# Weight products placed one pair earlier, their loads ahead of the small ones, and a block end without GpSimd's drain

## What is computed

```
w = weights[conditions]                        # per sequence, 64 x 64
u = einsum('bct,bcd->bdt', x, w)
x = x + selective_scan(u, ...)                 # 16 states per channel
a = attention(x)                               # paged keys/values, window 256, 8 heads, 4 groups
a = a @ Wo
scores = a @ w_r + b_r;  idx = top_k(scores, L/2)
h = gelu(a[idx] @ w1 + b1)
out = zeros.at[idx].set(h @ w2 + b2)
x = x + out
```

## Time and profile before

| | us |
|---|---|
| runs of the kernel: median of 3 (lowest, highest) | 1920.51 (1919.56, 1924.25) |
| the profiled execution, its own time | 1921.25 |
| its span, from first to last instruction | 1919.4 |
| PE busy in the span | 1828.5 (95%) |
| DVE, ACT, POOL busy | 1457.0, 1261.0, 1267.4 |
| mean granted TensorE clock (1.0 is 2.4 GHz) | 0.986 |

### The profile page before, as it was taken

The page is one execution under the profiler, slowest core; times in us unless marked ns, Lnnn a source line. Parts: engine busy times, 40 slices in busy tenths (PEclk is TensorE's granted clock), DMA queues, the critical chain, the costliest instruction groups (busy, mean ns, idle before and its releaser), DMA issues.

```text
span 1919.4 us, 29987 instructions
## 1 busy us (share of the span) xinstructions
PE 1828.5 (95%) x9311; PEld 1273.0 (66%) x9311; DVE 1457.0 (76%) x2572; ACT 1261.0 (66%) x3937; POOL 1267.4 (66%) x1253
## 2 busy tenths in 40 slices
PE   7899999999999999988599899999999999999998
PEld 6777777777777777765355575756657575665765
DVE  8999999999999999997455565655656565565522
ACT  5888888888888888865354674655646465564621
POOL 5789999999999999988677545444554544550000
PEclk8999999999999999999799999999999999999999
DMA  5423322333233323320776434434353343431021
GB/s 205 151 107 145 144 112 113 139 142 126 103 139 145 145 96 123 132 88 24 221 211 200 113 89 112 123 108 124 93 141 100 108 122 108 123 95 60 30 64 42
DMA packets 117069, 228.57 MB, mean 119 GB/s; under 512 B 31332, under 2 KB 70260, under 8 KB 111920
## 3 DMA queue, kind: packets, MB, share of 16 engines
q1 hardware_dynamic: 83824, 161.38, 23.8%
q0 software_dynamic: 33088, 65.28, 12.6%
HBM read 209.99 MB, written 44.70 MB: 133 GB/s over the span
## 4 chain that ended last, share of the span: by engine, by line
PE 46%; ACT 2%; issue 1%; DMA 1%; DVE 1%; POOL 0%; DVEq 0%; SPq 0%; ACTq 0%; POOLq 0%
PE attn_psum L1911 12%; PE attn_psum L1927 11%; PE attn_psum L1843 5%; PE attn_psum L1823 5%; PE attn_psum L1830 4%; PE attn_psum L1869 3%; PE attn_psum L1814 2%; PE attn_psum L1945 2%; PE attn_psum L1804 1%; PE attn_psum L1855 1%; ACT xh L1556 1%; ACT th L1557 1%; DMA kv_at<-kv_scratch,new_now 0%; ACT prob L1514 0%; ACT k_t L1504 0%
## 5 line engine op out<-in xcount | busy, mean ns | idle before, releaser
L996 DVE TENSOR_TENSOR_SCAN hid<-scan_psum,dbu 128x1024 f32<-128x1024 f32 x256 | 581.7, 2273 | 0.0
L1161 PE MATMUL scan_psum<-hid,ident 128*128 128x256 f32 x2048 | 520.3, 385 | 26.4 <-POOL hid L492 26.2
L1161 PEld LDWEIGHTS scan_psum<-hid,ident 128*128 128x128 f32 x2048 | 378.8, 191 | 188.9 <-issue 106.4
L1665 DVE CUSTOM_DVE_ANT_0 prob<-attn_psum,mask 128x336 f32<-128x336 f32 x256 | 120.1, 505 | 280.8 <-PE attn_psum L1823 280.5
L492 POOL TENSOR_TENSOR hid<-hid,kv_at 128x1024 f32<-128x1024 f32 x128 | 306.2, 2404 | 27.5 <-DVE hid L996 27.2
L492 POOL TENSOR_TENSOR hid<-hid,bc 128x1024 f32<-128x1024 f32 x128 | 306.0, 2403 | 23.2 <-DVE hid L996 22.8
L1520 ACT COPY p_t<-attn_psum 112x384 f32<-112x384 f32 x256 | 122.3, 484 | 285.4 <-PE attn_psum L1830 285.4
L1927 PE MATMUL attn_psum<-w,ffn_hid 128*128 128x512 f32 x512 | 238.5, 595 | 5.0 <-DVE y_sb L1730 5.0
L1446 POOL DMA_INDIRECT kv_at<-kv_scratch,new_now x189 | 200.5, 1061 | 63.6 <-issue 56.7
L1911 PE MATMUL attn_psum<-xs_in,w 128*128 128x256 f32 x1024 | 232.4, 381 | 7.5 <-ACT xs_in L1526 6.6
L635 ACT ACTIVATE scan_psum<-kv_at,neg_a 128x252 f32<-128x252 f32 x512 | 211.6, 466 | 13.9 <-DVE hid L996 12.3
(11 more groups left out here) (222 smaller groups left out, 3036.2 us busy)
## 6 DMA issues: line engine op xcount, KB each, us to landing
bc<-bc_scratch SPq DMA_DIRECT2D x16, 2048.0 KB, 7.4
kv_at<-bc_scratch SPq DMA_DIRECT2D x15, 2048.0 KB, 7.4
q_scratch<-qg SPq DMA_DIRECT2D x32, 260.0 KB, 2.0
early<-q_scratch SPq DMA_DIRECT2D x32, 260.0 KB, 3.5
x_pair<-in_x_pairs SPq DMA_DIRECT2D x32, 256.0 KB, 2.8
kv_scratch<-kvg SPq DMA_DIRECT2D x32, 256.0 KB, 2.1
a_scratch<-a_sb SPq DMA_DIRECT2D x32, 256.0 KB, 3.6
w_o<-x_scratch SPq DMA_DIRECT2D x32, 256.0 KB, 3.1
```

Of the source, the lines that this page charges most:

```text
L996: nc.vector.tensor_tensor_scan(hid[:, k % RING, :, :].rearrange("p n t -> p (n t)"), decay[k % 2], dbu[:, k % RING, :, :].rearrange("p n t ...
L1161: mm = nc.tensor.matmul(yc, ident[:], hid[:, k % RING, i, :], start=False, stop=(k % 4 == 3 and i == 3))
```

## The change

1. The scan's block is made with `no_gpsimd_drain=True`: GpSimd's drain at the end of that block is gone. The other engines' drains and the barrier stay.
2. Fold `n` stands in quarter `4 * m + w` in place of `4 * (m - 1) + w`: all folds come one pair earlier, fold 0 in w = 0 of pair 0, fold 16 in w = 0 of pair 4.
3. SyncE's list begins with `w_r` and `w_o`, on a semaphore of their own (`s_wo`), and `w1`'s part 0. The eight others follow, then part 1 of `w1`. Part `m + 1` (2 and 3) is loaded in pair `m` (1 and 2).
4. Fold 0 waits for `s_wo`; `s_late` counts eight loads.

```diff
-        block = ctx.enter_context(nc.Block())
+        block = ctx.enter_context(nc.Block(no_gpsimd_drain=True))
...
-        NC, NLATE = 3, 10
+        NC, NLATE = 3, 8
...
-            n = 4 * (m - 1) + w
+            n = 4 * m + w
             return n if 0 <= n < NFOLD else None
...
                     sp.wait_ge(pe_sc, 8 * m + 2)
-                    if m < NCH:
-                        load_w1(m)
+                    if m + 1 < NCH:
+                        load_w1(m + 1)
...
-            for dst, src in ((own, A["own"]), (before, A["before"]), (slot_no, A["slot_no"]), (w_o, A["w_o"]),
+            sp.dma_start(w_r[:], A["w_r"]).then_inc(s_wo, 16)
+            sp.dma_start(w_o[:], A["w_o"]).then_inc(s_wo, 16)
+            load_w1(0)
+            for dst, src in ((own, A["own"]), (before, A["before"]), (slot_no, A["slot_no"]),
                              (b1, A["b1"]), (slot_own, A["slot_own"]), (tok_no, A["tok_no"])):
                 sp.dma_start(dst[:], src).then_inc(s_late, 16)
-            sp.dma_start(w_r[:], A["w_r"]).then_inc(s_late, 16)
             sp.dma_start(b_r[:], A["b_r"].partition_broadcast(P)).then_inc(s_late, 16)
             sp.dma_start(b2[:], A["b2"].partition_broadcast(P)).then_inc(s_late, 16)
-            load_w1(0)
+            load_w1(1)
...
                 if n == 0:
-                    pe.wait_ge(s_late, 16 * NLATE)
+                    pe.wait_ge(s_wo, 32)
```

More of the change, by code:

```diff
@@ L1258, in attention_ffn_block @@
         s_c, s_late = W["a_const"], sem("a_late")
-        s_w, ld_w1 = sem("s_w_ffn"), [sem(f"ld_w1{i}") for i in range(2)]
+        s_wo, s_w, ld_w1 = sem("s_wo"), sem("s_w_ffn"), [sem(f"ld_w1{i}") for i in range(2)]
         pe_fold, act_fold = sem("pe_fold"), sem("act_fold")
```

## The result

The changed kernel takes 1914.24 us (median of 7 runs, 1913.47 to 1916.65), against 1920.51 of the kernel before: a ratio of 0.9964 (95% interval 0.9952 to 0.9975), so 6.3 us less (by the ratio 6.9, from 4.8 to 9.2). The whole interval lies on the side of a gain. The gain is just beyond the 0.3% (5.8 us) that the forecast took as its mark, with the interval on both sides of that mark. The median is 0.1 us from the forecast of 1914.1. The profiled execution has 1914.64 us of its own time and a span of 1912.8 (before 1921.25 and 1919.4); the mean granted clock is 0.991 (before 0.986).

A forecast was written before the change was run, and what follows sets the result against it. TensorE was taken to bound the attention block almost everywhere, except the gap with pair 0 and pair 5. Four folds in pair 0 (+4.1, drain gain included) and four fold-free quarters (-10.5) gave -6.4 us: 1914.1 us, range 1910.0 to 1918.5.

The forecast's parts named there:

- Step 1: End of the scan's block: removing GpSimd's drain, priced at 3.7 us, lets all engines start near 933.0.
- Step 2: Pair 0: four folds added, fold 0 partly at low clock, sequence 2's wait covered; pair 1's scores 4.1 us later.
- step 4: Reordered loads at the attention block's head: costed at nothing, with 0.8 us of cover for sequence 1's rows.
- Step 3: w = 1, 2, 3 of pair 4 and w = 0 of pair 5, without folds: 10.5 us earlier, bounds 8.1 to 12.6.
- The sum: Whole kernel: +4.1 - 10.5 = -6.4 us, the drain's gain inside; 1914.1 us forecast for the median.
- A: Gap between the blocks: entering a block costs the 4.3 us, not the drain; -2.7, 1917.8 us; chance 0.12.
- B: Pair 0: big loads crowd out the gathers, PE waits up to 3 us; -3.4, 1917.1 us; chance 0.12.
- C: Pair 0: the clock stays low throughout, up to 1935.9 us, slower than before; chance 0.06.

The follow-up runs named there:

- drain kept: The change with GpSimd's drain put back, folds and loads as in the change: 1917.26 us, ratio 0.9979 to the kernel before.
- part 1 late: The change with `w1`'s part 1 loaded in pair 0, quarter 1, not at the head: 1913.43 us, ratio 0.9958 to the kernel before.
- the run with thin folds in the kernel before: The kernel before with folds 13 to 16 cut to one of their four matmuls: 1912.45 us, ratio 0.9950.
- Even with thin folds: The change with folds 0 to 3, in pair 0, cut to one of their four matmuls: 1908.92 us, ratio 0.9934 to the kernel before.
- the loads alone: The kernel before with only the new load order, folds and drain as before: 2003.75 us, ratio 1.0019, on the odd chip alone.
- the even spread: The change with the 17 folds spread evenly over 24 quarters of pairs 0 to 5: 1912.84 us, ratio 0.9953 to the kernel before.

## Why the prediction was right

**Step 1, the drain: price right, gain capped.** 4.3 to 4.7 us from POOL's end to the first load with the drain (five kernels), 0.6 us behind SyncE's landing without: the 3.7 us of the forecast. The drain's own row gives 4.1 us behind POOL's last gather; the gap was labelled after all, by a row of POOL's sequencer, which the forecast did not use. All engines then start at 933.39, forecast 933.0. What the step left out is that the landing of SyncE's store stands right behind the drain. In the kernel before it came at 929.07 + 3.2 = 932.3, early enough for 933.0. In the changed kernel's execution POOL was 1.5 us sooner, but the store 0.4 us later, and it set the start. Against POOL's end and 4.4 us, the gain is 1.9 us in that execution and 3.0 in the run of the drain alone. The time says 2.5 (0.8 to 4.0), too wide to tell these apart. That the gathers just ahead make the drain long, which the step drew from the launch, is not borne out: without them it took 4.37 us.

**Step 2, four folds in pair 0: +5.0 in place of +4.1.** The mechanism held: fold 0 partly at the lower clock (5.5 us from its first matmul, forecast 5.5), no wait for sequence 2, three whole quarters behind it. From the end of fold 0 to pair 1's scores pass 20.0 us (950.58 to 970.56), forecast 20.1. The whole 0.9 us lies ahead of fold 0, which starts at 945.05 and not at 944.1: 0.4 from the later start and 0.5 from the wait for sequence 1's rows. There step 4 failed: it costed that wait at nothing with 0.8 us of cover, from landings of 3.3 to 6.4 us, and the gather took 7.6. That was in sight. The answer behind the earlier trace rows has the landings of six of the nine gathers; of the three it lacks, sequence 2's, the chain shows one with 7.67 us, and step 2 used it. With 7.67 sequence 1's rows land at 944.1, 0.5 us after PE, which is what came.

The clock rose at about 948.9, forecast 947.9. That this came so close is in part luck. The forecast took the distance from one row of scores to the rise, 6.2 us, from a single trace. In the ten traces from the other chips the distance from the same row runs from 4.0 us (drain kept: 944.55 to 948.6) to 7.5 (part 1 late: 942.47 to the end of this window), and is 6.9 in the changed kernel:

```profile
949.00:950.00 1.00, 1.00 (x2) 0.47 (x2) 0.00 (x0) 0.00 (x0) 0.70 (x2) 0.52 1.06 212
```

The allowance of 3.4 us either way covers that. *By the Trainium skill ("TensorE: Matmul & The Clock Gate", Part 4: transposes do not count) I had priced a rise 2.4 us after the forecast's, at 950.3.* The traces do not bear that out: with the drain kept the rise came about 1.5 us after fold 0's first matmul (0.70 in the window from 948 to 949), and with no fold in pair 0 at all it came too, in the kernel before and in the one with only the drain gone (0.85 in the window from 948 to 949). Nor do they refute the rule, since scores and values, which are no transposes, stand among the work ahead of it.

**Step 3, four quarters without a fold: -11.9 in place of -10.5.** The first three took 10.4 us, forecast 11.9; the last 5.25, forecast 5.1. The size that was off is w = 2: 3.5 taken, from pair 5 with its single bank, 2.3 measured with two. It lay within the bounds (up to 12.6), and the run with thin folds in the kernel before confirms the place: 9.6 us less for 10.9 us of work.

**The sum.** Steps 1 and 2 came out 0.9 worse and step 3 1.4 better than forecast, and pair 5 gave 0.5 back: the errors cancel. That the median came within 0.1 us is partly luck; each term by itself was right within 1.5 us. One sum of the forecast is off: added up in the same way as its lower end (1910.3), the upper end of its own spread is 1918.2 (1914.1 + 1.7 + 2.4) and not 1917; the range went to 1918.5 in any case.

**The rivals.** A is refuted by the gap of 1.4 us and by the drain's own row. B happened in small: 0.5 us at sequence 1, nothing at sequence 2, against the up to 3 us of its price. C did not: the grant was 1.00 from 949 on. Even with thin folds, where PE waits 1.60 us at sequence 2, pair 0 was not longer than without folds.

## What to carry to other kernels

When a wait at a barrier is removed, look up who is second to last: here the landing of another engine's store, and the 0.6 us behind it, left at most 1.9 to 3.0 of the drain's 4 us to gain. When the timeline has no name for a gap, the rows of the sequencers may have one: the drain stood there. When a landing time is taken from a row, see how many of the transfers that row covers. When fixed work is moved into a gap, measure the gap, not the list position: here the front held one fold's work for nothing and charged the rest about 85% by the traces, while the gain came from the end that was freed. That filler work is better spread over the quarters than put in a block is what the traces suggest (some 3 us), but the times do not show it.

## What the runs showed of the hardware

**A drain on GpSimd.** With three gathers of rows issued just ahead of it, it ended 4.1 to 4.5 us after the last of them, and the next block began 4.3 to 4.7 us after it. With the last gather 0.9 us back and none of new rows it took 4.37 us. At launch, with no gather before it, it took 0.19. In the kernel before DMA traffic was down to 21 GB/s in the window that ends 1.5 us before the drain does.

**Gathers beside large loads.** Sequence 1's gathers of new rows landed in 5.0 to 6.4 us in the kernel before and in 5.1 to 6.2 with only its drain gone; the last of them took 7.6 in the change and 7.5 with part 1 late, with 2 MB of loads issued ahead of it in place of 1. Sequence 2's took 7.3 to 7.7 in the change, and 8.5 to 9.0 in the kernel before with its drain gone, so they were not made slower by the new order. The 1 MB of `w_o`, issued ahead of the other large loads, took 5.1 us and the `w1` parts 9.8 and 16.0.

**TensorE's clock behind the idle start.** From the same row of scores to the rise from 0.50 to 1.00 passed 4.0 to 7.5 us in ten traces. With 3.9 us of it at the lower level, fold 0 of the change took 5.5 us in place of 3.6.

**Run to run.** The scan's last store was issued anywhere between 929.1 and 933.7 us in the profiled executions of these kernels, all with the same scan. Traces of two executions are therefore compared from the first load on, not by absolute times.

**A chip that is slower in one stage.** On the first chip the attention block was almost 80 us longer, with the same kernel. Windows of the kernel without the drain on it, against 143.32 us of PE in the same stretch of the kernel before on the chip of the forecast:

```profile
936.00:1092.00 156.00, 128.55 (x657) 72.52 (x658) 68.40 (x257) 67.95 (x189) 93.66 (x116) 0.85 0.58 166
```

Its chain holds pieces like these, which the profile can't name:

```profile
962.53 5.15 another core or an unknown queue
...
969.27 7.68 another core or an unknown queue
```

No experiment was aimed at it; its cause stays open. Also open are the loads alone, what a drain waits for, and whether the even spread beats the change.
